# A mixture-of-experts layer on one core: the weights of a sorted tile moved by a transfer instead of by ScalarE

## What is computed

```python
x = x + 0.5 * ffn(layernorm(x), Wg, bg, W1, b1, W2, b2)
x = x + attn(layernorm(x))
x = x + 0.5 * ffn(layernorm(x), Wg, bg, W1, b1, W2, b2)
# ffn: logits = x @ Wg + bg; softmax; the best 2 of 8 experts, weights made to sum to 1;
#      expert e: relu(x @ W1[e] + b1[e]) @ W2[e] + b2[e], with W1[e] 128x256 and W2[e] 256x128
# attn: 16 heads of 8 numbers, scores = centred x times itself, softmax over 512 tokens, times x
```

## Time and profile before

| what | value |
|---|---|
| median of 3 runs | 1019.02 us (1017.11 to 1022.14) |
| profiled execution, its span | 1039.1 us |
| PE busy in the profiled execution | 975.9 us, 94% of the span |
| ACT busy | 833.7 us, 80% |
| DVE busy | 789.0 us, 76% |
| ACT's copies into chosen | 56 instructions, 59.2 us |

### The profile page before, as it was taken

How to read it: one execution, slowest core, us unless ns; L and a number is a source line. 1 busy time by engine, 2 the same in 40 slices (tenths; PEclk the granted TensorE clock), 3 DMA queues, 4 the chain that set the end, 5 groups by cost and what they waited for, 6 DMA issues and landing times.

```text
span 1039.1 us, 20329 instructions
## 1 busy us (share of the span) xinstructions
PE 975.9 (94%) x6512; PEld 546.9 (53%) x6512; DVE 789.0 (76%) x2255; ACT 833.7 (80%) x1194; POOL 529.3 (51%) x623
## 2 busy tenths in 40 slices
PE   7899999999999999989999999998999998888995
PEld 5687777633332488843333323332688862246673
DVE  5799999867767789857777777776878754368997
ACT  4655553599999988879999999998999988865653
POOL 5546777744444314354677766666100006555775
PEclk8999999999999999999999999999999999899998
DMA  6444223000051234420111111261444421133443
GB/s 182 165 152 133 100 102 103 14 21 20 19 147 60 75 130 163 145 89 24 36 37 35 36 37 34 57 179 36 122 139 146 143 83 49 44 127 107 131 155 121
DMA packets 59821, 96.15 MB, mean 93 GB/s; under 512 B 9179, under 2 KB 30403, under 8 KB 59715
## 3 DMA queue, kind: packets, MB, share of 16 engines
q1 hardware_dynamic: 47568, 71.50, 21.5%
q0 software_dynamic: 10752, 22.04, 7.1%
q10 hardware_dynamic: 1396, 1.31, 0.4%
HBM read 56.36 MB, written 38.45 MB: 91 GB/s over the span
## 4 chain that ended last, share of the span: by engine, by line
PE 53%; ACT 18%; issue 11%; DVE 10%; POOL 3%; DMA 3%; another core or an unknown queue 1%; SPq 0%; ACTq 0%; POOLq 0%; DVEq 0%
ACT probs L2023 10%; PE ps L1764 10%; PE ps L1749 6%; ACT sums L2023 5%; DVE low L1007 3%; PE ps L1375 3%; PE ps L1377 3%; PE ps L1376 2%; PE ps L1361 2%; PE ps L1386 2%; PE ps L1387 2%; PE ps L1391 2%; PE ps L1398 2%; PE ps L732 2%; PE ps L734 2%
## 5 line engine op out<-in xcount | busy, mean ns | idle before, releaser
L2023 ACT ACTIVATE probs<-ps 128x1024 f32<-128x1024 f32 x344 | 337.1, 1126 | 20.4 <-PE ps L1749 20.0
L1704 POOL DMA_INDIRECT found<-tiles,home x168 | 168.2, 1001 | 198.7 <-ACT sums L2023 126.9
L1692 POOL DMA_INDIRECT sorted<-xn,slot x168 | 168.1, 1000 | 179.2 <-ACT probs L2023 63.0
L1764 PE MATMUL ps<-probs,value 128*32 128x512 f32 x1376 | 185.2, 610 | 3.1 <-ACT probs L2023 1.4
L2023 ACT ACTIVATE sums<-ps 128x1024 f32<-128x1024 f32 x168 | 173.8, 1127 | 7.8 <-PE ps L1749 6.9
L1749 PE MATMUL ps<-shared 32*128 32x512 f16 x1024 | 144.7, 387 | 20.5 <-ACT probs L2023 6.8
L1188 ACT ACTIVATE high<-ps 128x512 fp32r<-128x512 f32 x176 | 101.1, 593 | 74.3 <-PE ps L734 58.7
L1007 DVE SCALAR_TENSOR_TENSOR low<-ps,high 128x512 fp32r<-128x512 f32 x176 | 113.0, 682 | 11.2 <-ACT high L1188 10.2
L1749 PEld LDWEIGHTS ps<-shared 32*128 32x128 f16 x1024 | 37.9, 91 | 157.8 <-ACT probs L2023 72.1
L1264 POOL TENSOR_TENSOR sums<-sums 128x512 f32<-128x512 f32 x59 | 76.6, 1298 | 66.6 <-DVE sums L1039 48.5
L1764 PE MATMUL ps<-sums,value 128*32 128x512 f32 x672 | 90.9, 613 | 0.2 <-ACT sums L2023 0.2
(11 more groups left out here) (202 smaller groups left out, 1869.2 us busy)
## 6 DMA issues: line engine op xcount, KB each, us to landing
found<-sorted SPq DMA_DIRECT2D x56, 256.0 KB
tiles<-sums SPq DMA_DIRECT2D x56, 256.0 KB
probs<-gates SPq DMA_DIRECT2D x24, 512.0 KB
wide<-gates SPq DMA_DIRECT2D x20, 512.0 KB
sorted<-zeros SPq DMA_DIRECT2D x16, 512.0 KB
out<-X SPq DMA_DIRECT2D x15, 256.0 KB
sorted<-xn,slot POOLq DMA_INDIRECT x168
found<-tiles,home POOLq DMA_INDIRECT x168
```

The lines of the kernel that those rows point to most:

```text
L1692: nc.gpsimd.indirect_dma_start(sorted_rows[group_of(q)], bass.IndirectOffsetOnAxis(ap=slot[:, q % XNS, k, j:j + 1], axis=0), xn[:, rows_sl ...
L1704: nc.gpsimd.indirect_dma_start(found[:, q % 2, k, j, :], None, tile_rows[group_of(q)], bass.IndirectOffsetOnAxis(ap=home[:, q, k, j:j + 1] ...
L1764: ins = nc.tensor.matmul(ps[q * W:(q + 1) * W, MIX, :], value[:, s % 2, sd, j, m, q, :], ring[ring_at(g * UNITS + 2 * j + q // 2)][:, q % ...
L2023: nc.scalar.activation(ring[ring_at(n)], ps[:, score_banks(n), :], ACT.Exp, scale=SCORE).then_inc(sm["a_probs"], 1)
```

## The change

load_weights(t) on SP starts a transfer of the 512 KB from `weights` to `chosen`, both in SBUF; choose(t) on ACT keeps only the reading of the expert's number, which biased(t) needs. hidden(t) waits for the transfer's semaphore in place of the copy's. The order in SP's stream is new: the first three weights come behind the first two tile loads, and in slot i load_weights(i+2) comes ahead of load_tile(i+4) and store_tile(i-2).

```diff
+        tile_weights = sems("tile_weights", 3)
...
+            def load_weights(t):
+                if t in TILE0:
+                    sp.wait_ge(sm["g_expert"], tiles_of(t) + 1)
+                of = nc.sync.value_load(expert_of[0:1, tiles_of(t), tile_at(t):tile_at(t) + 1], min_val=0, max_val=E - 1)
+                reached(sp, sm["t_expert"], t - 2)
+                sp.dma_start(chosen[:, t % 3, :, :].rearrange("p k f -> p (k f)").bitcast(F32),
+                             weights[:, bass.ds(of, 1), :, :].rearrange("p a k f -> p (a k f)").bitcast(F32)).then_inc(tile_weights[t % 3], 16)
...
             def sync_stream(a, b, at_slot):
                 for t in range(a, a + 2):
                     load_tile(t)
+                for t in range(a, a + 3):
+                    load_weights(t)
                 for i in stream(a, b):
+                    if i > a and in_stream(i + 2, a, b):
+                        load_weights(i + 2)
                     if in_stream(i + 4, a + 2, b):
                         load_tile(i + 4)
                     if in_stream(i - 2, a, b):
...
             def hidden(t):
                 u = t % 2
-                pe.wait_ge(sm["t_weights"], t + 1)
+                pe.wait_ge(tile_weights[t % 3], 16 * (t // 3 + 1))
...
                 of[t] = nc.scalar.value_load(expert_of[0:1, tiles_of(t), tile_at(t):tile_at(t) + 1], min_val=0, max_val=E - 1)
-                reached(act, sm["t_expert"], t - 2)
-                nc.scalar.activation(chosen[:, t % 3, :, :].rearrange("p k f -> p (k f)"),
-                                     weights[:, bass.ds(of[t], 1), :, :].rearrange("p a k f -> p (a k f)"), ACT.Copy).then_inc(sm["t_weights"], 1)
```

More of the change, by code:

```diff
@@ L413, in build @@
  g_base g_zrowf g_zrow g_total g_count g_placed g_row g_home g_expert
- t_turned t_xh t_xl t_weights t_hidden t_high t_low t_expert t_y t_back t_out
+ t_turned t_xh t_xl t_hidden t_high t_low t_expert t_y t_back t_out
  c_half c_added
```

## The result

| | before | after |
|---|---|---|
| median of the runs compared | 1019.91 us (1015.95 to 1024.09, 17 runs) | 1023.69 us (1020.34 to 1031.85, 17 runs) |
| after to before | | 1.0043, 95% interval 1.0024 to 1.0062 |
| profiled execution: its own time, its span | span 1039.1 us | 1028.33 us, 1026.5 us |

The change costs 0.43% of 1020 us, 4.4 us, with an interval of 2.4 to 6.3 us. The ratio compares all the runs; it isn't the quotient of the two medians, which differ by 3.8 us. Of all the runs in this document two, of 1746 and 1991 us, were far slower than the rest and are left out of every ratio and mean. The change is a loss, smaller than the 0.5% (5.1 us) that were called no change, though the interval reaches beyond that; the median lies 3.6 us above the 1020.1 us of the prediction.

A forecast was written before the change was run, and what follows sets the result against it. PE was taken to set the streams' pace, hiding ACT's copy. Terms -0.6 (stream ends), +0.8 (second stream's head) and +0.9 (tile 36's slot) made +1.1 us on 1019.0: 1020.1 us, range 1015.5 to 1037 us.

The forecast's parts named there:

- What bounds the streams: Both streams: PE sets the pace at 3.67 us a tile, ACT's copy is hidden behind it; 0 us in running tiles.
- Rival C: Both streams: faster, if ACT is part of the pace or streams start sooner; 1014.7 us at best, chance 0.07.
- the two ends: Ends of both streams: PE no longer waits for copies there; -0.6 us, bounds 0 and 4.3 us.
- Release to use: Each tile's weight transfer: lands in 3.0 us, with 4.34 us from expert(t-3)'s end to hidden(t); 0 us per tile.
- upper bound of 4.25 us: Weight transfer's longest time: a 256 KB tile load's 3.03 us plus 1.22 us for another 256 KB, still just in time.
- Rival B: Running tiles: slower by latency alone once a transfer takes over 4.34 us; at 5.3 us +24 us, 1043 us, chance 0.08.
- the sum: Whole kernel: -0.6 at stream ends, +0.8 at second stream's head, +0.9 at tile 36's slot, making +1.1 us.
- The DMA engines: Both streams: each transfer costs 1.49 us of all 16 engines; shares rise to 0.85 and up to 0.93, and fit.
- rival A: Both streams: DMA engines become the pace; at twice the price +45 us, 1064 us, at 1.6 times 1034; chance 0.22.
- Head of the second stream, +0.8: Tile 27's load, behind three weight transfers, lands 0.8 us late; bounds 0 and 2 us.
- Slot of tile 36, +0.9: Tile 39's weights go out behind store_gates, landing 0.9 us after their use; bounds 0 and 2.2 us.
- SP's queue elsewhere: Running slots: SP's issues take 2.5 us of 3.67; loads and stores behind the waiting transfer are covered, no loss.

The follow-up runs named there:

- e4_no_loads_in_loop: Changed kernel without the weight transfers for all but each stream's first three tiles, so later tiles reuse old weights; 1022.69 us, 1.0017 of the kernel before.
- e7_twice: Changed kernel plus a second 512 KB transfer per tile, from weights to an HBM tensor nothing reads; 1065.88 us, 1.0445 of the kernel before.
- e1_head: Changed kernel with tile loads put ahead of the second and third weights at each stream's head; 1023.78 us, 1.0023 of the kernel before.
- e3_both: Changed kernel with tile loads put ahead of weights at each stream's head and store_gates one slot later; 1020.99 us, 1.0005 of the kernel before.
- e8_split: e3_both with each tile's transfer split into W1 and W2 halves, each with its own semaphore; 1027.83 us, 1.0083 of the kernel before.
- e9_split_order: e8_split with SP's order changed to W2 half, tile load, store, W1 half; 1021.81 us, 1.0026 of the kernel before.
- e12_split_order_again: The kernel of e9_split_order, unchanged, profiled once more; 1021.82 us, one execution.

## Why the prediction was right, point by point

- **What bounds the streams.** Right. PE stays at 10.00 of 10 us, and e4_no_loads_in_loop shows 3.66 to 3.68 us a tile with no copy and no transfer at all. Rival C had a small truth: tiles 39 to 52 take 0.27 us less, 3.67 in place of 3.69 us each, and the head of the first stream and the two ends give 1.3 us (-0.5, -0.5, -0.4) where -0.6 was counted, within the bounds of 0 to 4.3.
- **Release to use.** The estimate of 3.0 us is the smallest landing, 3.11 us the median of those that met no instruction packet. The upper bound of 4.25 us failed: 5.55 us was measured. Rival B was priced as a lateness of every tile; what came is a lateness of one to four tiles in an execution, by waits of 0.1 to 1.0 us, where a landing went beyond the budget of 4.34 us. That most landings stay within it was worked out; that single ones go beyond was not in the sum.
- **The DMA engines.** Right. In the ten us of the earlier trace rows the shares rose by 0.33 and 0.32 where 0.41 and 0.36 were counted, but over tiles 39 to 52 the share rose by 0.41, from 0.43 to 0.84, and over tiles 0 to 21 from 0.43 to 0.81. A tile's 128 packets of 4 KB take 1.39 to 1.45 us of all sixteen engines, near the 1.49 counted. Such a packet takes 160 ns by the median inside SBUF and 159 ns from HBM, so rival A's doubled price is out, and e7_twice shows where its point lies. The Trainium skill (DMA: Bandwidth & Descriptors, "Where 436 GB/s comes from") puts such a transfer at 435 GB/s, an estimate of 1.2 us for 512 KB; sixteen engines with 4096 bytes in 160 ns make 410 GB/s, 1.28 us, so by the median packet the trace agrees within a tenth. By the mean packet, 174 to 181 ns in the streams, it is the 1.39 to 1.45 us above, a fifth over the estimate.
- **Head of the second stream, +0.8.** The mechanism was right, the size was not: +2.1 and +5.0 (against 8.12). The third load went out 6.5 us after the first, not 5.56. It landed 2.8 us after its issue in one execution and 4.4 in the other, where a packet of q8 was under way; 3.03, "nothing more for the queue", was taken. The bound of 2 us for the wait failed at 2.60. A clock at half behind the wait was not foreseen at all. Of the 2.9 us between the two executions 1.5 lie ahead of tile 27's turn, which is the later landing, and 1.4 behind it, which is the fall from 733.5 on. The fall from 726.6 on shows no cost there, since PE idled 2.60 us for the load after it. e1_head and e3_both come to 8.7 to 8.9 us, the second with a fall like the one in the head of 8.92 of before.
- **Slot of tile 36, +0.9.** Right in place, low in size: +1.5 and +2.0. The weights of tile 39 landed 3.7 and 4.2 us after their issue, not 3.0; tile 38's, late too, is part of the first number.
- **SP's queue elsewhere.** Right: no tile load was late but that of tile 27. The count of 2.5 us of SP's time in 3.67 was right as well: in e3_both SP waits 17.4 of 56 us, which leaves it 2.5 us a tile. How near that is to its limit was not seen: one issue and one wait more per tile were enough in e8_split's order, though not in e9_split_order's.
- **What was missing.** The sum ended with the streams. The part behind them was put at nothing without a reason, and gave 0.6 to 2.9 us in the two executions; an instruction packet in a gather and, in the first, a fall of the clock behind it are what is seen there. Together: +1.1 plus the mis-sized terms (+1.3 to +4.2 at the head, +0.6 to +1.1 at tile 36, -0.7 at the ends) and this make about 4 to 8 us for the two executions (tile 3 of the second, late by 0.7, with them); over many runs 4.4 us were measured. That this is still below the 0.5% is in part luck: the places were right, but the loss is four times the +1.1 of the sum, and its interval reaches to 0.62%.

No version found here beats the kernel before. The best order makes the streams some 0.5 to 1.5 us faster, and that is less than what is lost behind them. That loss is explained in part only. e9_split_order is 0.26% or 2.7 us slower in all (interval 0.9 to 4.3) though its streams gain about 1 us, so some 3.6 us are lost outside them; the two gathers, without a fall of the clock, make 1.1 to 1.4 us. The rest stays open.

## What to carry to other kernels

Work taken from an engine that isn't the pace gives back next to nothing (here 1.6 us of 59); what it is replaced by has to fit everywhere, so look first where the order is written for something else: the head of a loop, and the slot with one extra issue. Compare a transfer's time to use with its slowest landing, not with the median, and give it a whole step of room: e9_split_order had landings of up to 4.7 us and no tile waited. Count the issuing engine's own time per step like any other engine's, register readings included, and after the change look at the parts that it does not touch.

## What the runs showed of the hardware

- Inside SBUF a 4 KB packet takes 160 ns of one DMA engine by the median, 159 ns from HBM to SBUF; the packets of 512 KB take 1.39 to 1.45 us of all sixteen engines; 512 KB land 3.0 to 3.3 us after their issue (smallest and median) and cost SP 0.50 us of issue.
- The profile counts instruction packets (q8, q14) with the work of the same sixteen DMA engines that move the data. The Trainium skill (Runtime: NRT & Kernel Launch, "Instruction fetch mechanics") says that the next block is fetched while the current one runs, so that the crossing is mostly hidden. For the program that is fetched no run shows otherwise. For the data a cost is seen, as a relation and not as a test: a transfer that meets such a packet landed in 3.65 to 4.09 us by the median in place of 3.11, and a gather that met one let ACT wait 2.1 to 2.6 us in place of 0.7 to 1.9.
- A part whose code is unchanged came out 0.6 to 3.3 us longer in every execution of the changed kernels than in the two later ones of before (the first one of before was longer than all, 189.5 us), and instruction packets lie at other places in it. That the packets move with the number of instructions is argued, not shown.
- The granted clock went from full to half for 3.4 us at a time behind idle times of PE of 2 to 3 us, in some executions and not in others with the same wait: ahead of the second stream's first turn it fell behind 2.02 us in e12_split_order_again and stayed full behind 2.15 in e9_split_order; before shows both as well, behind 2.16 and 2.11 us.
